# Moving two layer-norm tiles, two copies and one scaling between ScalarE and VectorE in a fused attention and FP4 feed-forward kernel

## What is computed

```
xn  = layernorm(x)
Q   = elu(xn Wq + bq) + 1 ;  K = elu(xn Wk + bk) + 1 ;  V = xn Wv + bv
o   = Q (K^T V) / (Q . sum(K) + eps)                  # linear attention, 16 heads of 64
x1  = layernorm(xn + o Wo + bo) * g1 + be1
s   = layernorm(x1 + gelu(x1 W1 + b1) W2 + b2) * g2 + be2
g   = silu(fp4_linear(silu(fp4_linear(xn, wg)) * fp4_linear(xn, wu), wd))
out = x + s * g
```

## Time and profile before

| | |
|---|---|
| Runs | 1679.47, 1679.61, 1681.95 us; median 1679.61 |
| Profiled execution, own time | 1680.37 us |
| Its span, first to last instruction | 1678.5 us |
| Granted TensorE clock, mean | 0.996 of full speed |
| TensorE matmul busy | 1644.1 us, 98% |
| TensorE weight loads busy | 1469.2 us, 88% |
| VectorE busy | 1322.8 us, 79% |
| ScalarE busy | 967.5 us, 58% |
| GpSimd busy | 778.4 us, 46% |

### The profile page before, as it was taken

How to read it: one execution, slowest core, us unless ns; L and a number is a source line. 1 busy time by engine, 2 the same in 40 slices (tenths; PEclk the granted TensorE clock), 3 DMA queues, 4 the chain that set the end, 5 groups by cost and what they waited for, 6 DMA issues and landing times.

```text
span 1678.5 us, 30547 instructions
## 1 busy us (share of the span) xinstructions
PE 1644.1 (98%) x11105; PEld 1469.2 (88%) x11105; DVE 1322.8 (79%) x2587; ACT 967.5 (58%) x1754; POOL 778.4 (46%) x718
## 2 busy tenths in 40 slices
PE   7999999999999999999999999999999999999997
PEld 6878888888889898989999998989898999999897
DVE  6685664555879797979889797979797988979797
ACT  6665656655464646565655556464646565555644
POOL 4564543434134444444453534444444446353446
PEclk9999999999999999999999999999999999999999
DMA  7322323422200101021010102010101201010100
GB/s 230 130 77 89 106 66 116 121 91 91 93 1 1 51 1 51 19 86 52 1 51 2 51 2 104 2 51 2 51 19 34 77 29 51 1 51 2 51 1 26
DMA packets 69986, 89.36 MB, mean 53 GB/s; under 512 B 8383, under 2 KB 54603, under 8 KB 68814
## 3 DMA queue, kind: packets, MB, share of 16 engines
q1 hardware_dynamic: 69838, 87.42, 15.9%
HBM read 53.30 MB, written 34.10 MB: 52 GB/s over the span
## 4 chain that ended last, share of the span: by engine, by line
PE 54%; DVE 12%; issue 4%; ACT 1%; POOL 1%; DVEq 0%; ACTq 0%
PE QH L81 7%; PE QH L83 6%; PE QH L82 6%; PE AC L81 6%; PE AC L83 6%; PE AC L82 6%; PE GU L81 4%; PE GU L83 4%; PE GU L82 4%; PE TT L816 3%; DVE hb L1760 1%; DVE bslna L1840 1%; DVE hb L1758 1%; PE QH L714 1%; DVE AC L1831 1%
## 5 line engine op out<-in xcount | busy, mean ns | idle before, releaser
L1212 ACT ACTIVATE rh<-QH 128x512 fp32r<-128x512 f32 x256 | 147.1, 595 | 84.2 <-DVE QH L1918 80.1
L81 PE MATMUL GU<-wgh,xqh 128*128 128x352 f32 x512 | 171.2, 334 | 8.9 <-DVE hb L1760 8.8
L2416 POOL TENSOR_TENSOR hb<-hb,rs_h 128x704 f32<-128x704 f32 x64 | 89.1, 1392 | 170.0 <-DVE rs_h L1767 170.0
L82 PE MATMUL GU<-wgl,xqh 128*128 128x352 f32 x512 | 165.7, 324 | 0.0
L83 PE MATMUL GU<-wgh,xql 128*128 128x352 f32 x512 | 165.6, 323 | 0.0
L1933 DVE TENSOR_TENSOR rl<-QH,rh 128x512 fp32r<-128x512 f32 x128 | 85.7, 689 | 95.1 <-ACT rh L1212 74.7
L81 PE MATMUL AC<-Mh,rh 128*128 128x256 f32 x512 | 145.7, 285 | 0.0
L81 PE MATMUL AC<-w2h,rh 128*128 128x256 f32 x512 | 144.2, 282 | 0.0
L82 PE MATMUL AC<-Ml,rh 128*128 128x256 f32 x512 | 142.8, 279 | 0.0
L83 PE MATMUL AC<-Mh,rl 128*128 128x256 f32 x512 | 142.7, 279 | 0.0
L82 PE MATMUL AC<-w2l,rh 128*128 128x256 f32 x512 | 142.4, 278 | 0.0
(11 more groups left out here) (241 smaller groups left out, 5711.1 us busy)
## 6 DMA issues: line engine op xcount, KB each, us to landing
xa<-in_L_attn_src SPq DMA_DIRECT2D x16, 512.0 KB, 4.2
xt_scratch<-xth SPq DMA_DIRECT2D x32, 256.0 KB, 2.6
xt_scratch<-xtl SPq DMA_DIRECT2D x32, 256.0 KB, 3.0
xb<-in_L_attn_src SPq DMA_DIRECT2D x16, 512.0 KB, 4.2
xnTh<-xt_scratch SPq DMA_DIRECT2D x32, 256.0 KB, 4.7
xnTl<-xt_scratch SPq DMA_DIRECT2D x32, 256.0 KB, 5.4
out<-x SPq DMA_DIRECT2D x15, 512.0 KB, 6.6
m_scratch<-mh SPq DMA_DIRECT2D x16, 256.0 KB, 2.4
```

The source lines that it names most:

```text
L81: e.matmul(outp, lh, rh, start=start, stop=False, skip_group_check=check)
L82: e.matmul(outp, lh, rl, start=False, stop=False, skip_group_check=check)
L1212: e.activation(RH[j % 4][:], src, ACT.Copy).then_inc(S[sem], 1)
L2416: e.tensor_tensor(hb, hb, spread(rs_h[i % 2][:], 44), ALU.mult).then_inc(S["hin"], 1)
```

## The change

Three things are moved, and two small buffers are added in a space that was kept free behind the other tiles, so that no other address changes.

1. The first norm. Tiles 0 and 1 of each group are normed by ScalarE, behind `gate_tanh(c, 0)`, as scale times input plus bias; the bias is minus the mean times the reciprocal root, which `ln1_rstd` on GpSimd makes with two more multiplications for the first pair. VectorE norms tiles 2 and 3 only, and does so behind `gate_mul(c, 0)` and no longer ahead of it. The semaphore `lnan` now counts ScalarE's two norms, `lnad` VectorE's two, and `lnab` the bias.
2. `gelu_hi(g, 5)` and `gelu_hi(g, 6)` stand on ScalarE directly behind `gelu(g, 5)` and `gelu(g, 6)`; before, both came behind the second gelu, `h_abs(d)` and `x_norm(g + 1, 2)`. On VectorE `gelu_lo(g, 5)` stands ahead of `x_max(g + 1, 0)` for groups before the last.
3. The high part `zhi` of the reciprocals is written by VectorE at the end of `den_inverse`; `z_sign` is gone from ScalarE.

The core of the diff; the calls are changed in the same way for group 0, for group 1 and in the loop:

```diff
-            def z_sign(g):
-                w.wait_ge(S["zi"], 2 * g + 2)
-                w.wait_ge(S["sel"], 6)
-                w.wait_ge(S["zd"], 4 * g)
-                e.activation(zhi[:], dn_s[:], ACT.Identity, scale=sg[:, 1:2]).then_inc(S["zc"], 1)
+            def ln1_norm(g, t):
+                w.wait_ge(S["lnap"], 2 * g + 1)
+                w.wait_ge(S["lnab"], g + 1)
+                e.activation(x1[g % 2][:, t, :], AC[:, t * D:(t + 1) * D], ACT.Identity, bias=nmb1[:, t:t + 1],
+                             scale=rsb["lna"][:, t:t + 1]).then_inc(S["lnan"], 1)
...
                 gate_tanh(a + 4, 0)
-                z_sign(g + 1)
                 gate_tanh(b + 4, 0)
...
                 gate_tanh(c + 4, 0)
+                ln1_norm(g + 1, 0)
+                ln1_norm(g + 1, 1)
                 x1_hi(g + 1, 0)
...
                 gelu(g + 1, 5)
+                gelu_hi(g + 1, 5)
                 gelu(g + 1, 6)
+                gelu_hi(g + 1, 6)
                 h_abs(d + 4)
                 if g + 2 < NG:
                     x_norm(g + 2, 2)
-                gelu_hi(g + 1, 5)
...
-            def ln1_norm(g, pr):
-                w.wait_ge(S["lnap"], 2 * g + pr + 1)
-                for t in (2 * pr, 2 * pr + 1):
+            def ln1_norm(g):
+
+                w.wait_ge(S["lnap"], 2 * g + 2)
+                for t in (2, 3):
                     e.tensor_scalar(x1[g % 2][:, t, :], AC[:, t * D:(t + 1) * D], mvb["lna"][:, t, 0:1], rsb["lna"][:, t:t + 1],
-                                    ALU.subtract, ALU.mult).then_inc(S["lnan"], 1)
+                                    ALU.subtract, ALU.mult).then_inc(S["lnad"], 1)
...
                 e.reciprocal(dn_s[:], dn_s[:]).then_inc(S["zi"], 1)
+                w.wait_ge(S["zi"], 2 * g + 2)
+                w.wait_ge(S["sel"], 6)
+                e.tensor_scalar(zhi[:], dn_s[:], sg[:, 1:2], None, ALU.mult).then_inc(S["zc"], 1)
...
+                gelu_lo(g, 5)
                 x_max(g + 1, 0)
-                gelu_lo(g, 5)
                 gelu_lo(g, 6)
...
-                ln1_norm(g + 1, 0)
-                ln1_norm(g + 1, 1)
                 gate_mul(c + 4, 0)
+                ln1_norm(g + 1)
...
                 e.tensor_tensor(rsb["lna"][:, tiles], vt["lna"][:, tiles], nhalf[:, 0:2], ALU.pow).then_inc(S["lnap"], 1)
+                if pr == 0:
+                    e.tensor_tensor(nm1[:, 0:2], mvb["lna"][:, tiles, 0], neg4[:, 0:2], ALU.mult).then_inc(S["lnam"], 1)
+                    w.wait_ge(S["lnap"], 2 * g + 1)
+                    w.wait_ge(S["lnam"], g + 1)
+                    e.tensor_tensor(nmb1[:, 0:2], nm1[:, 0:2], rsb["lna"][:, tiles], ALU.mult).then_inc(S["lnab"], 1)
```

More of the change, by code:

```diff
@@ L52 @@
     "x1Tl", "gel", "lna", "lnb", "fin",
-    "hin", "hout", "xin", "xout", "lnap", "lnbp", "lnav", "lnbv", "lnbs", "us", "xab", "xnb", "vb2", "half", "fo", "lastp",
+    "hin", "hout", "xin", "xout", "lnap", "lnam", "lnab", "lnad", "lnbp", "lnav", "lnbv", "lnbs", "us", "xab", "xnb", "vb2", "half", "fo", "lastp",
     "wraw", "wk0", "wk1", "bk", "wgr0", "wgr1", "wgr2", "wdr", "vec", "row", "wqr", "wv", "x0", "x1", "x2", "m0", "m1", "ksr", "ksl", "kst", "xb0", "xb1", "xs0", "xs1", "xtl", "mld", "out0", "out1",
@@ L198, in build @@
         Xb = [Xb0, sb("xb1", [128, 4, D])]
-        sb("main_rest", [128, 682])
+        nm1, nmb1 = sb("nm1", [128, 8]), sb("nmb1", [128, 8])
+        sb("main_rest", [128, 666])
         A2 = ExitStack()
@@ L747, in f_step @@
                 w.wait_ge(S["A_wsl"], WSL[3])
-                w.wait_ge(S["lnan"], 4 * g + 4)
+                w.wait_ge(S["lnan"], 2 * g + 2)
+                w.wait_ge(S["lnad"], 2 * g + 2)
                 if g < NG - 1 or j < 6:
@@ L762, in turn_x1 @@
                 o = QH[:, pr * 512:(pr + 1) * 512]
-                w.wait_ge(S["lnan"], 4 * g + 2 * pr + 2)
+                if pr:
+                    w.wait_ge(S["lnad"], 2 * g + 2)
+                else:
+                    w.wait_ge(S["lnan"], 2 * g + 2)
                 w.wait_ge(S["zh"], 8 * g + 7 + pr)
@@ L1387, in _ @@
             gate_tanh(0, 0)
-            z_sign(0)
             gate_tanh(1, 0)
@@ L1405, in _ @@
             gate_tanh(2, 0)
+            ln1_norm(0, 0)
+            ln1_norm(0, 1)
             x1_hi(0, 0)
@@ L1427, in _ @@
             gelu(0, 5)
+            gelu_hi(0, 5)
             gelu(0, 6)
+            gelu_hi(0, 6)
             h_abs(3)
             x_norm(1, 2)
-            gelu_hi(0, 5)
-            gelu_hi(0, 6)
             g_tanh(1)
@@ L1451, in _ @@
             gate_tanh(4, 0)
-            z_sign(1)
             gate_tanh(5, 0)
@@ L1476, in _ @@
             gate_tanh(6, 0)
+            ln1_norm(1, 0)
+            ln1_norm(1, 1)
             x1_hi(1, 0)
@@ L1498, in _ @@
             gelu(1, 5)
+            gelu_hi(1, 5)
             gelu(1, 6)
+            gelu_hi(1, 6)
             h_abs(7)
             x_norm(2, 2)
-            gelu_hi(1, 5)
             for g in range(1, NG - 1):
                 a, b, c, d = 4 * g, 4 * g + 1, 4 * g + 2, 4 * g + 3
-                gelu_hi(g, 6)
                 g_tanh(b)
@@ L1576, in _ @@
                     x_norm(g + 2, 2)
-                gelu_hi(g + 1, 5)
             g_tanh(NT - 3)
-            gelu_hi(NG - 1, 6)
             h_hi(NT - 2, 0)
@@ L1835, in ln1_stats @@
                 w.wait_ge(S["lnap"], 2 * (g - 1) + pr + 1)
-                w.wait_ge(S["lnan"], 4 * (g - 1) + 2 * pr + 2)
+                if pr:
+                    w.wait_ge(S["lnad"], 2 * g)
+                else:
+                    w.wait_ge(S["lnab"], g)
                 w.wait_ge(S["lna"], v + 1)
@@ L2147, in _ @@
             ln1_stats(0, 1)
-            ln1_norm(0, 0)
-            ln1_norm(0, 1)
             gate_mul(2, 0)
+            ln1_norm(0)
             xT_half(0, 0, "x1T", "x1Th", "x1Tl")
@@ L2168, in _ @@
             h_round(2)
+            gelu_lo(0, 5)
             x_max(1, 0)
-            gelu_lo(0, 5)
             gelu_lo(0, 6)
@@ L2232, in _ @@
             ln1_stats(1, 1)
-            ln1_norm(1, 0)
-            ln1_norm(1, 1)
             gate_mul(6, 0)
+            ln1_norm(1)
             xT_half(1, 0, "x1T", "x1Th", "x1Tl")
@@ L2439, in ln1_rstd @@
                 w.wait_ge(S["lna"], 10 * g + 5 * pr + 5)
-                w.wait_ge(S["lnan"], 4 * (g - 1) + 2 * pr + 2)
+                if pr:
+                    w.wait_ge(S["lnad"], 2 * g)
+                else:
+                    w.wait_ge(S["lnan"], 2 * g)
                 w.wait_ge(S["cp"], 5)
```

## The result

| | before | changed |
|---|---|---|
| Median (runs) | 1679.57 us (4) | 1669.74 us (4) |
| Lowest and highest | 1679.47, 1681.95 | 1668.97, 1670.89 |
| Profiled execution | 1680.37 us | 1668.97 us |
| Its span | 1678.5 us | 1667.2 us |
| Granted TensorE clock | 0.996 | 0.998 |

The ratio is 0.9938, interval 0.9922 to 0.9953: 9.8 us less by the medians, 11.4 between the profiled executions. The forecast was 12.5 us less (1667.1), with a range of 1662 to 1673. The sign and the range were right, and the time came out 2.6 us above the forecast.

What follows compares the result with a forecast made beforehand. TensorE was taken as the bound, its matmuls covering 98% of the span. Gains of 5.1, 3.8 and 4.0 us less 0.4 made 12.5; from 1680.37 that gave 1667.9, and 0.76 lower for the median, 1667.1 us; range 1662 to 1673.

Steps and rivals of the forecast that it cites:

- TensorE bound, three stalls a group: Main loop: matmuls cover 98% of the span, so only TensorE's three stalls in each 77.9 us group can pay.
- A: Gate's load behind the transposes of normed tiles: splitting the norms gains 0.32 us per group, 16 times, 5.1 us.
- the slower rival: ScalarE's two norms become what everything waits for; a loss past 1.15 us each, 1690.6 us at 1.5 each; chance 0.02.
- B: Wait for gelu_lo(5) ahead of the last h projection: 0.40 us gained, 0.15 given back, net 0.25, 15 times, 3.8 us.
- x_round had 0.2 in hand, so q_elu(1) moves by 0.52: Chain to q projection 3: x_abs moves 0.32 us earlier, x_round's slack adds 0.2, so q_elu(1) comes 0.52 earlier.
- C: Second gate wait, behind the reciprocals: zhi on VectorE takes 0.30 us for 0.55, gaining 0.25 per group, 4.0 us.
- I take 0.23, nearer the VectorE row: Price of zhi's 128-column VectorE instruction: 0.23 us, between bounds 0.18 and 0.41; the row was 44 columns at 0.179.
- zhi meets GpSimd: Rival: a 2.4 us GpSimd instruction blocks zhi, adding up to 2 us per group, 1700 us or more; chance 0.01.
- The last group: The last tile's later abs delays the rounding ahead of gelu_lo(5): a loss of 0.4 us (0 to 1.0), once.
- What the profile would show: Signs: fewer gate waits, none for h projection 7's low part or zhi, small waits for x norms and q_elu(1), 77.1 us groups.
- The gate waits: TensorE's 32 waits for a gate's second product (8.8 us) fall to about 16, about 0.1 us each.
- the wait for q_elu(1): New TensorE wait at q projection 3 of 0.15 us (0 to 0.35).

Runs made afterwards that it cites:

- e1: The kernel before with only the norms' split (part 1 of the change): 1675.48 us, ratio 0.9978.
- e3: The kernel before with only zhi moved to VectorE (part 3 of the change): 1676.81 us, ratio 0.9989.
- e4: The changed kernel with GpSimd's x_in ahead of x1_residual and VectorE's x_scale ahead of gelu_lo(7): 1664.59 us, ratio 0.9917.
- e11: The kernel of e5 run again in rounds, nothing edited: 1665.03 us, ratio 0.9906.
- e2: The kernel before with only the high parts of gelu blocks 5 and 6 behind their gelus (part 2): 1679.58 us, ratio 0.9994.
- e12: The changed kernel run again, nothing edited: 1669.52 us, ratio 0.9943.
- e9: The changed kernel with TensorE's transposes of x turned tile by tile, each tile's waiting for its own norm alone: 1666.01 us, ratio 0.9910.
- e5: The changed kernel with only VectorE's x_scale moved ahead of gelu_lo(7), GpSimd's order left as it was: 1662.92 us in one run.
- e7: e4 with VectorE's h_max of tile a moved from ahead of the reciprocals to behind tile b's gate product: 1676.86 us, ratio 0.9984.
- e8: e7 with all four norms on ScalarE: 1679.1 us, ratio 1.0000.

## Why the prediction was right, point by point

- **TensorE bound, three stalls a group.** Right. With those stalls cut, a group went from 77.87 to 77.22 and 77.14 in two profiled executions: 0.65 and 0.73 of the 0.82 that the terms add up to. e1 to e3 show that each part works on one stall alone.
- **A, 0.32 per group.** Right: 0.33 by the starts, 0.34 by e1. The second pair of norms was expected to start 0.08 ahead of the gate product's end and did (1003.70 and 1003.78). ScalarE's norm, the unknown price, was taken as 0.596 from the SBUF row and measured 0.564; the slower rival needed 1.15.
- **B, 0.40, less 0.15.** The mechanism was right, down to the instruction that GpSimd holds, and the net was too large: 0.25 forecast, 0.16 measured. The stall itself gave 0.44. What came back was 0.28, inside the bounds of 0 to 0.35 but nearly twice the term. 0.20 of it is the wait at q projection 3. The step "x_round had 0.2 in hand, so q_elu(1) moves by 0.52" was a little off: counted from the first transposes' load, q_elu(1) ended at 32.52 before and at 32.05 with the change, 0.47 earlier, while TensorE came 0.77 earlier and not 0.72. The other 0.08 is the slower pace of the products behind that wait, which the working had no term for. e4 and e11 confirm the size: with q_elu(1) on time, both are gone.
- **C, 0.25.** The term was too large: 0.17 to 0.19. The step that failed is "I take 0.23, nearer the VectorE row". zhi took 0.285, nearer the middle of its bounds (0.18 and 0.41), because 128 columns were priced by a row of 44. The trace before has an instruction of the same form and width, though from PSUM: `dn_s` ahead of the reciprocal, and it takes 0.28 before and after.
- **zhi meets GpSimd.** It didn't: all 16 took 285 to 288 ns.
- **The last group, -0.4.** Wrong: from the last first transpose to the end took 45.78 us before and 45.77 in e2, which has this part of the change alone. (It took 45.39 with all of it and 45.43 in e1, which is the last group's stall A.) The late abs of the last tile was covered too, so this term was 0.
- **The sum.** With the measured terms it is 16 x 0.33 + 15 x 0.16 + 16 x 0.19 = 5.3 + 2.4 + 3.0 = 10.7 us, against 10.5 at one clock and 9.8 and 9.4 by the medians. The forecast of 12.5 had 0.2 too little for A, 1.4 too much for B, 1.0 too much for C, and at the end a loss of 0.4 that didn't come. That the errors at A and at the end went against the other two is luck. The rest, down to the medians, is of the size of what single executions of one kernel differ by (1667.67 to 1671.51 in e12).
- **What the profile would show.** The gate waits were to fall to 16 of 0.1; the list shows one, since the rest of stall C, a start 0.67 behind the two z_spread matmuls, isn't put down as idle by the profile. The other signs were as forecast, but the wait for q_elu(1) shows in start times only.

## What to carry to other kernels

When a wait holds a batch of instructions, ask which of them need what came last: letting six of eight transposes go (e9) bought 0.2 us a group for no work at all, a third of what the whole change did. An instruction that another engine blocks is free if it stands where its engine would idle anyway, so it should be put in the hole and not behind it (e5, e11). Taking work from an engine pays only where a stall ends with that engine; the same reduction in another place (e7) cost what the change had gained.

## What the runs showed of the hardware

- Closely spaced matmuls of 256 columns ran at one of two distances, 0.113 or 0.118 us, a whole stretch at a time. The level behind q projection 3 went with the order of work (0.118 in 60 of 60 groups with a late q_elu(1), in 3 of 150 without); the level of a group's last stretch differed between executions of one kernel (0.113 in 15 of 15 groups of e5, in 2 of 15 of e11). Over the main phase the mean was 0.1148 to 0.1155, which is worth up to 3 us in an execution.
- TensorE's granted clock fell to 0.50 in three places. In 12 of 14 profiled executions it did so for 3.4 us (in four of them 6.8), starting between 45.6 and 48.5 us, where TensorE had been busy without a break (7.00 of the 7.00 us from 40.9 to 47.9 in the changed kernel). In three (before, e7, e8) it did so near 441 us, where it had stood still for nearly half of the four microseconds before. In all 14 it did so for the last 2.7 to 5.8 us, where TensorE had no matmul left (none in 5.7 us in the kernel before). In the first two places each 3.4 us cost 1.0 to 1.3.
- A VectorE tensor_scalar of 0.18 us took 0.74 and 2.36 us beside a GpSimd product of 2.4 us, and the next one got in before the next product, which started 0.08 us after the first had ended.
- ScalarE's scale-and-bias form took 564 ns from PSUM and 596 ns from SBUF for the same 128 by 256 elements: reading PSUM was the cheaper of the two.
